# Newton steps through a PSUM bank, a second round in small pieces between shared steps, and the late table among the tiles

## The chip, the cores and the metric

The kernel runs on one core of one Trainium2 chip. Its metric is the device time of one execution, in microseconds. A core has five engines with queues of their own: TensorE (PE), VectorE (DVE), ScalarE (ACT), GpSimd (POOL) and SyncE (SP), the last used for DMAs. Each works through its instructions in the order in which they are written and waits only on semaphores.

## What is computed

One pre-norm transformer layer on 2048 tokens of width 128:

```
x = x + attention(layernorm(x))        # 16 heads of 64, causal, softmax, output projection
x = x + ffn(layernorm(x))
ffn(x): shared = (silu(x @ sg.T) * (x @ su.T)) @ sd.T
        probs = softmax(x @ gate_w.T); topw, topi = top_k(probs, 2); topw /= topw.sum
        out = shared + sum over the two chosen of 8 experts of topw * expert(x)
```

The hidden width of every expert is 352. The kernel keeps the accuracy of fp32 by splitting numbers into a high and a low part, so a product is three matmuls (`mm3`).

## The kernel before

**Attention.** Each of 16 heads has 20 slots, one for each pair of key tiles of a block of 512 queries. A slot n is: scores on TensorE into `st`, two exponentials on ScalarE (fp32 and fp16), `p_low` on GpSimd (L583, the difference of the two), and on TensorE the products with v of slot n - 3. `exps(n)` waits until products n - 5 are done, scores n until exponentials n - 2 are. `normalise` on VectorE ends a block (slots 1, 5, 11, 19), and the first product of the next block waits for it. Between scores and products each slot takes *background tasks*, each on TensorE into one of three banks `bg`, drained by VectorE in the same order (`bg_ready`, `bg_drained`). `LAST_HEAD` places those of head 15: `att_t`/`att_y` (output projection of a block), `turn` (tokens to partitions, statistics), `rows_t` (normalised rows back), `logits`. Their consumers on VectorE are `inverse_deviation` (reciprocal root by two Newton steps, operations of 8 elements, lines L805 to L816), `normal_rows` (L824) and `second_copy` (a copy of the rows for the second expert).

**Router.** Twice, for 1024 tokens each: ScalarE's exp, `router_top` (L849 to L867), `router_weights`, `ranks` and `places` (where each row goes). Then GpSimd's `scatter_rows` writes the rows of that half to memory, sorted by expert, with 16 indirect DMAs (L611).

**Shared expert.** Twelve steps q: two times three products into `st`, silu on ScalarE, `hidden` (L1064) on VectorE, high part on ScalarE, low part `hidden_lo` (L1070) on VectorE, and `down` of step q - 2 on TensorE (L1152 to L1154 are the products). Between the steps the rest of the last head's tasks, the second round of the router and the tables stand in an order written by hand. `early_table` gives the rows and experts of tiles 0 to 8, which need the first scatter only, `late_table` those of the other 30.

**Tiles.** 39 tiles of 128 rows of one expert: SyncE gathers (L498), TensorE transposes (L1393), makes six products (L1403 to L1408), transposes silu's product (L1417) and multiplies down (L1426, L1430); VectorE and ScalarE work between; GpSimd stores each result (L618). A gather waits for the store eight tiles before. At the end SyncE loads the stored rows (L503), VectorE adds them (L1143, L1145), SyncE stores the output (L507).

## Time and profile before

| | us |
|---|---|
| median of 3 runs (lowest, highest) | 1005.98 (1005.53, 1006.03) |
| profiled execution | 999.62 |
| its span | 997.8 |
| TensorE, VectorE, ScalarE, GpSimd busy | 935.9, 741.6, 713.4, 729.9 |
| mean granted TensorE clock (share of full) | 0.954 |

The profile is of one execution. Its times count from the start of the span. A row gives start, length, engine, line, operation and operands; an engine's idle time before the row and what ended it stand in square brackets. Instructions of one engine overlap a little, so the next can start before the row before it ends.

### The profile page before, as it was taken

Reading aid. Unit: us, or ns where it says so; the run is one execution under the profiler, and the core shown is the slowest. Engines: PE = TensorE matmul, PEld = TensorE weight load, DVE = VectorE, ACT = ScalarE, POOL = GpSimd, SP = SyncE. Lnnn points to the kernel's source line nnn. Section 1 sums busy time; section 2 is a strip of 40 time slices with the busy share of each in tenths; the row PEclk is TensorE's granted clock in tenths of the full one; section 3 lists DMA queues with packets and bytes.
Section 4 is the critical chain, followed back from the end, with each engine's and each line's share of the span. In section 5 each row is a group of like instructions: output and inputs, shape, how many; then the busy total and the mean of one; then the engine's idle time right before and its main releaser. Section 6 shows DMA issues by size and latency. Waiting matters only on the chain. (4 is left out here: it accounts for less than half of the span.)

```text
span 997.8 us, 25979 instructions
## 1 busy us (share of the span) xinstructions
PE 935.9 (94%) x10330; PEld 793.1 (79%) x10330; DVE 741.6 (74%) x1775; ACT 713.4 (71%) x891; POOL 729.9 (73%) x460
## 2 busy tenths in 40 slices
PE   7889999999999999999999999999999976679992
PEld 6558888888888888888888888888888765569992
DVE  4978696868778786878697869686876478656664
ACT  3038888888788788788878788888888853426661
POOL 1328878888888889888988897888789956154442
PEclk7769999999999999999999999999999979879996
DMA  3321434343534344444522241404030306011214
GB/s 104 84 53 34 94 77 115 80 108 77 117 78 108 79 116 94 110 89 112 108 75 66 75 93 41 111 29 102 1 87 5 133 6 249 25 49 57 58 55 134
DMA packets 70103, 82.03 MB, mean 82 GB/s; under 512 B 8784, under 2 KB 53970, under 8 KB 67936
## 3 DMA queue, kind: packets, MB, share of 16 engines
q1 hardware_dynamic: 67712, 76.14, 31.0%
q0 software_dynamic: 2272, 4.24, 1.2%
q8 instruction: 84, 1.38, 0.6%
q14 instruction: 35, 0.29, 0.1%
HBM read 21.81 MB, written 25.30 MB: 47 GB/s over the span
## 5 line engine op out<-in xcount | busy, mean ns | idle before, releaser
L583 POOL TENSOR_TENSOR p_lo<-prob,p_hi 128x1024 f16<-128x1024 f32 x320 | 617.2, 1947 | 144.8 <-ACT p_hi L685 143.5
L684 ACT ACTIVATE prob<-st,p_bias 128x1024 f32<-128x1024 f32 x320 | 330.0, 1031 | 131.2 <-PE st L1276 106.8
L685 ACT ACTIVATE p_hi<-st,p_bias 128x1024 f16<-128x1024 f32 x320 | 328.1, 1025 | 0.0
L979 DVE TENSOR_REDUCE row_max<-bg 128x1 f32<-128x512 f32 x384 | 255.7, 686 | 15.8 <-PE bg L1201 10.8
L1275 PE MATMUL st<-big 128*128 128x512 f32 (+3 forms) x640 | 246.8, 386 | 2.5 <-ACT p_hi L685 1.6
L1300 PEld LDWEIGHTS pv<-v_parts,p_hi 128*128 128x128 f16 x2176 | 198.1, 96 | 56.8 <-issue 33.3
L1201 PE MATMUL bg<-big 128*128 128x512 f32 (+3 forms) x640 | 240.2, 407 | 2.7 <-DVE v_parts L969 2.1
L1300 PE MATMUL pv<-v_parts,p_hi 128*128 128x65 f16 x2176 | 236.6, 195 | 1.8 <-POOL p_lo L583 1.8
L1276 PE MATMUL st<-big 65*128 65x512 f32 (+3 forms) x640 | 236.3, 369 | 0.0
L1302 PE MATMUL pv<-v_parts,p_hi 128*128 128x64 f16 x2176 | 234.1, 195 | 0.0
L1304 PE MATMUL pv<-v_parts,p_lo 128*128 128x65 f16 x2176 | 232.4, 192 | 0.0
L1304 PEld LDWEIGHTS pv<-v_parts,p_lo 128*128 128x128 f16 x2176 | 203.2, 99 | 0.0
L1302 PEld LDWEIGHTS pv<-v_parts,p_hi 128*128 128x128 f16 x2176 | 202.9, 97 | 0.1
L1201 PEld LDWEIGHTS bg<-big 128*128 128x128 f32 x640 | 122.4, 195 | 29.1 <-DVE row_max L979 7.5
L1275 PEld LDWEIGHTS st<-big 128*128 128x128 f32 x640 | 122.9, 192 | 17.5 <-ACT p_hi L685 2.8
L1276 PEld LDWEIGHTS st<-big 65*128 65x128 f32 x640 | 122.2, 191 | 16.5
L975 DVE CUSTOM_DVE_ANT_0 junk<-bg,mask_wide 128x128 bf16<-128x128 f32 (+3 forms) x256 | 122.1, 484 | 10.7 <-PE bg L1201 10.5
L959 DVE TENSOR_SCALAR big<-bg,qk_bias 128x512 fp32r<-128x512 f32 x64 | 48.0, 750 | 72.8 <-PE bg L1154 72.7
L618 POOL DMA_INDIRECT y_dram<-p_lo,v_parts x39 | 37.8, 970 | 46.6 <-DVE p_lo L1123 46.6
L1280 PE MATMUL st<-mask_cols_r,ident_r 128*128 128x128 f32 x256 | 61.1, 239 | 0.0
L1280 PEld LDWEIGHTS st<-mask_cols_r,ident_r 128*128 128x128 f32 x256 | 49.2, 192 | 2.8
L961 DVE SCALAR_TENSOR_TENSOR big<-bg,qk_bias,big 128x512 fp32r<-128x512 f32 x64 | 48.1, 751 | 2.3
(224 smaller groups left out, 1214.4 us busy)
## 6 DMA issues: line engine op xcount, KB each, us to landing
big<-big SPq DMA_DIRECT2D x192, 128.0 KB, 2.3
row_dram<-fill SPq DMA_DIRECT2D x8, 1300.0 KB, 9.2
big<-part_dram SPq DMA_DIRECT2D x8, 1088.0 KB, 7.9
big<-big SPq DMA_DIRECT2D x16, 512.0 KB, 4.3
part_dram<-stage_parts SPq DMA_DIRECT2D x32, 176.0 KB, 2.6
part_dram<-stage_parts SPq DMA_DIRECT2D x16, 192.0 KB, 3.7
stage_raw<-ffn_w SPq DMA_DIRECT2D x16, 176.0 KB, 3.0
v_parts<-row_dram SPq DMA_DIRECT2D x39, 65.0 KB
```

Of the source, the lines that this page charges most:

```text
L583: nc.gpsimd.tensor_tensor(o, a, b, ALU.subtract).then_inc(p_lo_ready, 1)
L684: nc.scalar.activation(o32, src, ACT.Exp, bias=p_bias[:], scale=D ** -0.5)
L685: nc.scalar.activation(o16, src, ACT.Exp, bias=p_bias[:], scale=D ** -0.5).then_inc(exp_done, 1)
L975: nc.vector.tensor_tensor_reduce(masked[k % BGRING][:, 0:width], bank[:, 0:width], mask_wide[:, BLK - width:BLK], 1.0, -3.0e38, ALU.add, A ...
L979: nc.vector.tensor_reduce(row_max[:, t, c:c + 1], bank, AX_X, ALU.max).then_inc(bg_drained, 1)
L1201: mm = nc.tensor.matmul(bank[:, 0:width], q_hihi[s][:, tile(t)], k_lohi[s][:, c * BLK:c * BLK + width], start=True, stop=True)
L1275: nc.tensor.matmul(out, k_lohi[s][:, tile(kt)], q_hihi[s][:, q], start=True, stop=False)
L1276: mm = nc.tensor.matmul(out, k_hi_one[s][0:D + 1, tile(kt)], q_lo_shift[s][0:D + 1, q], start=False, stop=not diagonal)
L1280: mm = nc.tensor.matmul(st[:, n % STRING, k, tile(j)], ident_r[:], mask_cols_r[:], start=False, stop=True)
L1300: nc.tensor.matmul(out, p_hi[:, n % PRING, cols], v[:, 0:D + 1], start=(kt == 0 and j == 0), stop=False, skip_group_check=True)
L1302: nc.tensor.matmul(out[:, 0:D], p_hi[:, n % PRING, cols], v[:, D + 1:VW], start=False, stop=False, skip_group_check=True)
L1304: mm = nc.tensor.matmul(out, p_lo[:, n % PRING, cols], v[:, 0:D + 1], start=False, stop=(kt == 4 * b + j), skip_group_check=True)
```

## The change

In words:
- The Newton steps write their squares and a copy of the operand into the bank of the last `turn`, so that each two-input operation has one input in PSUM; the bank is given back after them. `inverse_deviation` is called inside `turn` 1 and `turn` 3.
- In the last head `rows_t 0` and 1 go from slots 13 and 15 to 15 and 17, `second_copy` to 13 and 14, `logits 0` from 16 to 19, and `turn 2` comes from the shared stage into slot 18. `router_exps(0)` and `router_top(0)` come after the last slot, on VectorE behind the last `normalise`.
- In the shared stage the rows of blocks 2 and 3 are normalised by ScalarE, the low parts of steps 6, 7 and 8 are GpSimd's, between its two scatters, and tasks, copies and the early table stand at other steps. `base 2` comes before the last low part.
- The late table is cut into three pieces behind the first three tiles.
- Blocks 1 and 3 of the final loads and stores are issued by ScalarE's queue.

The diff, without declarations:

```diff
@@ -54,8 +54,8 @@
              9: [("att_t", PAIRS - 1, 1)], 10: [("att_y", PAIRS - 1, 1)], 11: [("turn", 1)],
-             13: [("rows_t", 0)], 15: [("rows_t", 1)], 16: [("att_t", PAIRS - 1, 2), ("logits", 0)],
-             17: [("att_y", PAIRS - 1, 2)]}
+             15: [("rows_t", 0)], 16: [("att_t", PAIRS - 1, 2)], 17: [("att_y", PAIRS - 1, 2), ("rows_t", 1)],
+             18: [("turn", 2)], 19: [("logits", 0)]}
 STAGE_SLOTS = (9, 15)
@@ -132,8 +132,9 @@
 PROLOGUE += [("v", 0, q) for q in range(4)] + max_tasks(0) + [("shift", 0)]
-TAIL = [("ranks", 0), ("att_t", PAIRS - 1, 3), ("att_y", PAIRS - 1, 3), ("turn", 2), ("turn", 3), ("rows_t", 2),
-        ("rows_t", 3), ("base", 0), ("logits", 1), ("base", 1), ("ranks", 1), ("base", 2), ("base", 3)]
+TAIL = [("ranks", 0), ("att_t", PAIRS - 1, 3), ("att_y", PAIRS - 1, 3), ("turn", 3), ("base", 0), ("rows_t", 2),
+        ("rows_t", 3), ("logits", 1), ("base", 1), ("ranks", 1), ("base", 2), ("base", 3)]
+POOL_LOW = (6, 7, 8)
 STAGED = [(e, j) for e in range(EXPERTS) for j in range(3)]
@@ -388,6 +394,13 @@
             return slice(8 * g, 8 * g + 8)
+
+        def wait_hidden_low(eng, q):
+
+            if q in POOL_LOW:
+                eng.wait_ge(h_lo_pool, POOL_LOW.index(q) + 1)
+            elif q >= 0:
+                eng.wait_ge(h_lo_ready, sum(x not in POOL_LOW for x in range(q + 1)))
@@ -621,9 +632,17 @@
+            def hidden_low(q):
+                pool.wait_ge(h_hi_ready, q + 1)
+                wait(pool, down_done, q - HRING + 1)
+                nc.gpsimd.tensor_tensor(h_lo[q % HRING], h32[q % HRING], h_hi[q % HRING], ALU.subtract
+                                        ).then_inc(h_lo_pool, 1)
+
             pool.wait_ge(filled, 16 * FILLS)
-            for g in range(2):
-                scatter_rows(g)
+            scatter_rows(0)
+            for q in POOL_LOW:
+                hidden_low(q)
+            scatter_rows(1)
             for i in range(TILES):
@@ -700,8 +719,6 @@
                     exps(h, n)
-                    if h == H - 1 and n == 17:
-                        router_exps(0)
                     if n in STAGE_SLOTS and 0 <= 2 * (h - STAGE_FROM) < len(STAGED):
@@ -721,6 +738,16 @@
+            def normal_rows(b):
+
+                act.wait_ge(ln_scale, 1)
+                act.wait_ge(bg_drained, drained(("turn", b)))
+                for t in range(4 * b, 4 * b + 4):
+                    last = nc.scalar.activation(attn[:, t, 0:P], res[:, tile(t)], ACT.Identity, bias=shift_mean[:, t - 8:t - 7],
+                                                scale=rstd[:, t:t + 1])
+                last.then_inc(ln_rows, 1)
+
+            router_exps(0)
             for q in range(STEPS):
@@ -728,9 +755,13 @@
                     shared_copy((q - 5) // FC)
-                if q in (4, 5):
-                    turned_copy(q - 2)
-                if q == 8:
+                if q == 4:
+                    normal_rows(2)
+                    normal_rows(3)
+                if q == 5:
+                    turned_copy(2)
+                    turned_copy(3)
+                if q == 7:
                     router_exps(1)
@@ -763,6 +794,14 @@
                     tile_y_low(i - 2)
+            for k in range(YRING):
+                act.wait_ge(y_stored[k], 16 * len(range(k, TILES, YRING)))
+            for b in (1, 3):
+                act.dma_start(y_rows[:, 4 * b:4 * b + 4], y_back[:, 4 * b:4 * b + 4]).then_inc(y_landed[b], 16)
+            for b in (1, 3):
+                act.wait_ge(out_ready, b + 1)
+                act.dma_start(out_view[:, 4 * b:4 * b + 4, :], res[:, blk(b)].rearrange("p (t d) -> p t d", d=P)
+                              ).then_inc(out_stored, 16)
@@ -808,14 +847,24 @@
                                             ALU.mult, ALU.add))
+                wide = bg[:, NUMBER["turn", 2 * g + 1] % BGRING, :]
+                square, copy = wide[:, 0:8], wide[:, 8:16]
                 y = newton[:, 1]
                 for k, step in enumerate(RSQRT_STEPS):
-                    own(nc.vector.tensor_tensor(newton[:, 0], y, y, ALU.mult))
-                    own(nc.vector.tensor_tensor(newton[:, 0], newton[:, 0], var_half[:], ALU.mult))
+                    own(nc.vector.tensor_copy(copy, y))
+                    own(nc.vector.tensor_tensor(square, copy, y, ALU.mult))
+                    own(nc.vector.tensor_tensor(square, square, var_half[:], ALU.mult))
                     out = newton[:, 2] if k == 0 else rstd[:, t]
-                    own(nc.vector.scalar_tensor_tensor(out=out, in0=newton[:, 0], scalar=step, in1=y,
-                                                       op0=ALU.add, op1=ALU.mult))
+                    last = nc.vector.scalar_tensor_tensor(out=out, in0=square, scalar=step, in1=y, op0=ALU.add,
+                                                          op1=ALU.mult)
+                    if k == 0:
+                        own(last)
                     y = out
+                last.then_inc(bg_drained, 1)
+                dve.wait_ge(bg_drained, drained(("turn", 2 * g + 1)))
+                if g:
+                    nc.vector.scalar_tensor_tensor(out=shift_mean[:], in0=mean_var[:, t, 0], scalar=-1.0, in1=rstd[:, t],
+                                                   op0=ALU.mult, op1=ALU.mult).then_inc(ln_scale, 1)
@@ -907,13 +956,15 @@
-            def table(lo, n):
-
+            def table_bases():
                 own(nc.vector.tensor_scalar(gap[:, EXPERTS:EXPERTS + 1], end_tile[:, EXPERTS - 1:EXPERTS], -1.0, None,
                                             ALU.mult))
                 own(nc.vector.scalar_tensor_tensor(out=row_base, in0=gap, scalar=float(P), in1=region[:], op0=ALU.mult,
                                                    op1=ALU.add))
                 own(nc.vector.tensor_tensor(row_step, row_base[:, 1:EXPERTS + 1], row_base[:, 0:EXPERTS], ALU.subtract))
+
+            def table(lo, n):
+
                 by = ends_by[:, 0:n]
@@ -928,23 +979,25 @@
-            def early_table():
+            def early_bases():
                 tiles_counted(ALU.is_ge, 1)
                 running_ends()
                 own(nc.vector.tensor_scalar(gap[:, 0:EXPERTS], first_tile, -1.0, None, ALU.mult))
                 own(nc.vector.tensor_scalar(taken, first_tile, -1.0, float(EARLY), ALU.mult, ALU.add))
                 own(nc.vector.scalar_tensor_tensor(out=taken, in0=taken, scalar=0.0, in1=n_tiles, op0=ALU.max, op1=ALU.min))
-                table(0, EARLY)
-
-            def late_table():
+                table_bases()
+
+            def late_counts():
                 dve.wait_ge(table_ready, 1)
                 tiles_counted(ALU.is_gt, 0)
                 own(nc.vector.tensor_tensor(n_tiles, n_tiles, taken, ALU.subtract))
                 running_ends()
+
+            def late_bases():
                 own(nc.vector.tensor_tensor(gap[:, 0:EXPERTS], taken, first_tile, ALU.subtract))
-                table(EARLY, TILES - EARLY)
+                table_bases()
@@ -997,11 +1050,15 @@
                     last.then_inc(ln_stats, 1)
-                    nc.vector.tensor_copy(res[:, blk(b)], bank).then_inc(bg_drained, 1)
+                    copied = nc.vector.tensor_copy(res[:, blk(b)], bank)
+                    if b % 2 == 0:
+                        copied.then_inc(bg_drained, 1)
                     dve.wait_ge(ln_stats, b + 1)
                     for t in range(4 * b, 4 * b + 4):
                         last = nc.vector.bn_aggr(mean_var[:, t, :], stats[:, t, :])
                     own(last)
+                    if b % 2:
+                        inverse_deviation(b // 2)
                 elif task[0] == "rows_t":
@@ -1047,20 +1104,16 @@
                         background_task(task)
-                    if h == H - 1 and n == 11:
-                        inverse_deviation(0)
-                        normal_rows(0)
-                    if h == H - 1 and n == 12:
-                        normal_rows(1)
-                    if h == H - 1 and n in (14, 17):
-                        second_copy(0 if n == 14 else 1)
+                    if h == H - 1 and n in (11, 12):
+                        normal_rows(n - 11)
+                    if h == H - 1 and n in (13, 14):
+                        second_copy(n - 13)
+            normalise(H - 1, NG - 1)
             router_top(0)
-            normalise(H - 1, NG - 1)
             router_weights(0)
-            background_task(("ranks", 0))
             def hidden(q):
                 dve.wait_ge(silu_done, q + 1)
-                wait(dve, h_lo_ready, q - HRING + 1)
+                wait_hidden_low(dve, q - HRING)
                 nc.vector.tensor_tensor(h32[q % HRING], silu[q % SRING], st[:, q % 2, 1, :], ALU.mult
@@ -1072,39 +1125,36 @@
                 hidden(q)
-                if q:
+                if q and q - 1 not in POOL_LOW:
                     hidden_lo(q - 1)
                 if q == 0:
+                    background_task(("ranks", 0))
                     background_task(("att_t", PAIRS - 1, 3))
                 if q == 1:
                     background_task(("att_y", PAIRS - 1, 3))
                 if q == 2:
-                    background_task(("turn", 2))
                     background_task(("turn", 3))
                 if q == 3:
-                    inverse_deviation(1)
-                    normal_rows(2)
-                    normal_rows(3)
+                    early_bases()
                 if q == 4:
+                    table(0, EARLY)
+                if q == 5:
+                    background_task(("base", 0))
                     background_task(("rows_t", 2))
-                if q == 5:
                     background_task(("rows_t", 3))
+                if q == 6:
+                    background_task(("logits", 1))
                     second_copy(2)
+                if q == 7:
                     second_copy(3)
-                if q == 6:
-                    background_task(("base", 0))
-                    background_task(("logits", 1))
-                if q == 7:
-                    early_table()
                 if q == 8:
                     background_task(("base", 1))
                     router_top(1)
                 if q == 9:
                     router_weights(1)
                     background_task(("ranks", 1))
+            background_task(("base", 2))
             hidden_lo(STEPS - 1)
-            background_task(("base", 2))
-            late_table()
             background_task(("base", 3))
@@ -1137,6 +1187,12 @@
                     tile_y(i - 2)
+                if i == 0:
+                    late_counts()
+                if i == 1:
+                    late_bases()
+                if i == 2:
+                    table(EARLY, TILES - EARLY)
             for b in range(NB):
@@ -1361,22 +1417,20 @@
                     ).then_inc(gu_ready, 1)
+                if q == 2:
+                    background_task(("att_y", PAIRS - 1, 3))
                 if q >= FLAG:
                     down(q - FLAG)
-                if q == 0:
+                if q == 1:
                     background_task(("ranks", 0))
                     background_task(("att_t", PAIRS - 1, 3))
-                if q == 1:
-                    background_task(("att_y", PAIRS - 1, 3))
                 if q == 2:
-                    background_task(("turn", 2))
                     background_task(("turn", 3))
-                if q == 4:
+                if q == 5:
+                    background_task(("base", 0))
                     background_task(("rows_t", 2))
-                if q == 5:
                     background_task(("rows_t", 3))
                 if q == 6:
-                    background_task(("base", 0))
                     background_task(("logits", 1))
```

## Rows read from the trace of the kernel before

**Rows 1.** Stretches: busy us of each engine (instructions), clock, DMA share, GB/s.
```profile
782.00:826.20 44.20, 34.90 (x470) 29.55 (x469) 30.47 (x94) 29.69 (x32) 30.77 (x16) 0.88 0.08 28
826.20:892.50 66.30, 45.72 (x210) 35.53 (x206) 46.50 (x174) 20.75 (x36) 27.39 (x27) 0.85 0.28 101
892.50:985.20 92.70, 86.63 (x623) 83.68 (x622) 57.07 (x155) 53.62 (x155) 43.42 (x45) 0.96 0.18 52
```

**Rows 2.** Waits, 780 to 830 us: who waited for whom, total us, times, longest.
```profile
POOL p_lo L583 <- ACT p_hi L685: 13.0, 6, 7.9
...
PE bg L1228 <- DVE attn L824: 6.2, 1, 6.2
```

**Rows 3.** GpSimd in order of time, last head: start us, us, instruction [idle before].
```profile
795.16 3.26 POOL L583 TENSOR_TENSOR p_lo<-prob,p_hi 128x1024 f16<-128x1024 f32 x2 [1.27 <-ACT p_hi L685]
799.59 4.21 POOL L583 TENSOR_TENSOR p_lo<-prob,p_hi 128x1024 f16<-128x1024 f32 x2 [1.17 <-ACT p_hi L685]
811.65 6.47 POOL L583 TENSOR_TENSOR p_lo<-prob,p_hi 128x1024 f16<-128x1024 f32 x3 [7.85 <-ACT p_hi L685]
...
822.66 3.24 POOL L583 TENSOR_TENSOR p_lo<-prob,p_hi 128x1024 f16<-128x1024 f32 x2 [0.40 <-ACT p_hi L685]
```

**Rows 4.** VectorE in order of time, the first deviation's Newton steps.
```profile
797.45 0.99 DVE L805 TENSOR_SCALAR var_half<-mean_var 128x8 f32<-128x8 f32 x1
...
799.77 1.98 DVE L813 TENSOR_TENSOR newton<-newton 128x8 f32<-128x8 f32 x1
801.78 2.04 DVE L814 TENSOR_TENSOR newton<-newton,var_half 128x8 f32<-128x8 f32 x1
...
804.06 2.14 DVE L824 TENSOR_SCALAR attn<-res,mean_var,rstd 128x128 f32<-128x128 f32 x8
```

**Rows 5.** VectorE in order of time: router rounds, then the late table.
```profile
820.72 1.62 DVE L851 TENSOR_TENSOR pr<-pr,pr_sum 128x64 f32<-128x64 f32 x1
...
868.27 0.21 DVE L849 TENSOR_REDUCE pr_sum<-pr 128x8 f32<-128x64 f32 x1
...
886.53 0.28 DVE L897 SCALAR_TENSOR_TENSOR wo_all<-w_raw,iota_row 128x128 f32<-128x128 f32 x1
...
891.25 0.68 DVE L1020 TENSOR_TENSOR res<-res,bg 128x512 f32<-128x512 f32 x1
```

**Rows 6.** One source line: minimum, median and maximum ns of one instruction.
```profile
L824 DVE TENSOR_SCALAR attn<-res,mean_var,rstd x16: 331/340/586, 804.1 to 846.6; 128x128 f32<-128x128 f32 x16
```

**Rows 7.** TensorE in order of time, shared stage and start of the tiles.
```profile
834.79 0.39 PE L1152 MATMUL st<-xn_hi,shared_hi 128*128 128x512 f32 x1
...
835.49 0.40 PE L1152 MATMUL pv<-split,shared_hi 128*128 128x512 f32 x1
...
872.47 0.56 PE L1243 MATMUL bg<-wo_all,tri 128*128 128x64 f32 x2 [3.69 <-issue]
...
892.28 0.45 PE L1393 MATMUL pv<-ident,v_parts 128*128 128x128 f32 x1 [2.62 <-DVE shared_hi L1112]
```

**Rows 8.** VectorE in order of time, first tiles; then the end.
```profile
897.15 0.52 DVE L1132 TENSOR_TENSOR prob<-prob,st 128x352 f32<-128x352 f32 x1 [1.25 <-ACT prob L759]
...
898.55 0.52 DVE L1132 TENSOR_TENSOR prob<-prob,st 128x352 f32<-128x352 f32 x1 [0.22 <-ACT prob L759]
...
901.07 0.52 DVE L1132 TENSOR_TENSOR prob<-prob,st 128x352 f32<-128x352 f32 x1 [0.77 <-ACT prob L759]
...
989.21 0.69 DVE L1143 TENSOR_TENSOR res<-res,big 128x512 f32<-128x512 f32 x1 [6.87 <-DMA big<-y_dram]
```

**Rows 9.** GpSimd in order of time: second scatter's first instruction, first tile's store.
```profile
879.03 0.97 POOL L611 DMA_INDIRECT row_dram<-attn,place_u  x1 [25.24 <-DVE place_u L893]
...
901.09 0.97 POOL L618 DMA_INDIRECT y_dram<-p_lo,v_parts  x1 [1.47 <-DVE p_lo L1123]
```

**Rows 10.** SyncE's queue in order of time, from 884 us: start us, us, issues.
```profile
904.05 64.84 SPq L498 DMA_DIRECT2D v_parts<-row_dram  x31
985.37 2.03 SPq L503 DMA_DIRECT2D big<-y_dram  x4
```

12 lines of the change are left out of this document (7 added, 5 removed).

## The prediction

> **What bounds the kernel now.** I read the table of stretches first, then the waits around the last head, then each engine in order of time. The profiled execution took 999.62 us, of which 997.8 are the span; the runs have a median of 1005.98, 6.4 above it. All terms below are differences worked out from the one trace, and I subtract their sum from both totals alike.
>
> The change touches nothing before 797 us, slot 11 of the last head. Three stretches are open [rows 1]: the end of the last head (44.2 us, TensorE busy 34.9, its mean granted clock 0.88), the shared expert (66.3 us, busy 45.7, clock 0.85), and the tiles (92.7 us, busy 86.6). So TensorE bounds the tiles alone. In the last head GpSimd sets the pace, since a full p_low takes it 2.1 us (two in 4.21) without a pause when it is fed; and it sat idle for 13.0 us waiting for exponentials, 7.9 of them at once [rows 2, 3]. Behind that lies one chain: the Newton steps hold up `normal_rows`, TensorE stands 6.2 us in slot 13 before the transposes of `rows_t 0` [rows 2], no scores are made, ScalarE and then GpSimd run dry. The reader is to see why the steps are long: eight-element operations take 0.17 us, but L805 took 0.99 and ended when GpSimd's operations of 795.16 did (798.42), L813 took 1.98 and L814 2.04, each ending as one of the two of 799.59 ended [rows 3, 4]. The same happens to L851 in the first router round, 1.62 us [rows 5]. I read it as VectorE waiting for a GpSimd instruction to let go of the memory side they share.
>
> The page "SBUF — State Buffer" of the Trainium skill, section "Who interferes with whom", says so: a VectorE operation with two SBUF inputs, or a copy or tensor_scalar in a two-port mode, is fully blocked by a GpSimd instruction that reads SBUF, for that instruction's length. The trace agrees, with the numbers above. The rule also speaks against this change: it leaves the copies and tensor_scalars from SBUF to SBUF exposed, which is the first rival below.
>
> **Last head.** Newton's products now have one input in a PSUM bank. Each of the two rounds of steps costs one extra copy of 0.2 us, so eight operations, 1.6 us, where six took 4.9 (three of 0.2 before 799.77, then until 804.06); L805's 0.99 stays. `normal_rows(0)` starts at 800.8 instead of 804.06. `rows_t 0` goes from slot 13 to 15, so scores 14 and 15 are issued before it: exponentials 12 and 13 allow them (GpSimd had both by 801.7, the second of its operations of 799.59), and GpSimd's operations 14 and 15 run from 803.8 to 808.1 without the 7.85 us hole [rows 3]. What VectorE must finish next is `normal_rows` 0 and 1 (eight L824, 2.14 together [rows 4]), two `second_copy` (0.6 each), then `normalise` of block 2 (0.6), for which the product of slot 15 waits. Four cases of this:
> If nothing is held by GpSimd, they end by 804.8, GpSimd loses 0.65 us, and its last operation ends at 817.5 instead of 825.9 [rows 3]; the stage ends near 818.1, 8.1 us earlier than 826.2.
> If each L824 waits out one GpSimd operation, four of them take until 808.1, when GpSimd has no more input; the rest follows at its free speed, block 2 is normalised at 811.0, scores 16 come at 812.8, GpSimd goes on at 814.9 and the stage ends at 822.9: 3.3 us earlier, at worst 2.5 if the clock falls again as it did after the 6.2 us stall.
> The L824 have no wait between them, last 0.34 each and start 0.26 apart (eight in 2.14) [rows 4, 6], so the next has begun before the last is over. If they thus pass as one batch, GpSimd loses 2.1 us for the eight L824 and about one more for the copies, and block 2 is normalised at 807.7; with scores 16 at 809.5 GpSimd's operations 16 to 19 end by 819.2: 6.7 us earlier.
> If PSUM operands wait as well, it is as in the second case. I take 6.0, between the first three, and keep 2.5 and 8.1. `turn 2` and `logits 0` in slots 18 and 19 cost TensorE 2.3 us under GpSimd's pace; they would be on the path only if GpSimd were no longer the bound. The exponentials of the router leave this stage's ScalarE for nothing.
>
> **Shared expert.** I walk it from its first product (826.24 before), as offsets. The lengths are six products 1.4, three 0.7 (834.79 to 835.49 at the high clock), a full-width VectorE operation 0.6 to 0.7, a router top free of GpSimd 4.1 (868.27 to the ranks' start at 872.47) [rows 5, 7].
> Lost: `router_top(0)` used to run under the last p_lows and now comes after the last `normalise`; with its weights VectorE is free at 5.7 instead of 2.0. TensorE waits for it at 4.7 (ranks 0 are behind the second step now); attention's transposes and products follow to 10.5, against 7.8 before.
> Won: one `turn` (1.8 us of VectorE) has left the stage, and eight L824 (2.4 us, until 846.9) are ScalarE's. The walk gives `turn 3` at 12.2, its Newton steps until 17.3, ScalarE's rows until 20.6 (0.27 each), and sixth step at 20.8 against 23.4. From here each step waits for the low part of the one before it: down 3 at 23.2, base 0 and both `rows_t` until 25.5, their ScalarE and VectorE copies until 27.9, logits 1 until 30.6. Two hidden parts before the router are GpSimd's; its first scatter ends at 8.3 + 20.6 = 29, before they are asked for at 33, so they hide. ScalarE's exp stands one step earlier, so its two table loads delay step 8's silu to 36.7; down 6 is issued at 37.9, as before (38.0). `router_top(1)` ends at 43.9 instead of 46.2: 2.3 us won. I bound this walk by plus 1.6 and minus 2.3 (nothing won), its largest unproved piece (down 2 waits at 18.7 for VectorE behind `turn 3`, 3 us of idle TensorE in which the clock may fall; its mean in this stage was 0.85 [rows 1]).
> Behind it the order is ranks 1, two steps, the last downs. The late table, 886.53 to 891.25, stands between the last low part and VectorE's answer to the first tile; TensorE waited 2.62 us for that before the tile of 892.28 [rows 5, 7]. It is worth 4.7 if all of it is on the path (the last downs and `base 3` run beside it, so 3.1 at least); `base 2` ahead of the last low part gives some 0.9 more: 5.6 for both, 3.1 the low bound. Stage: 2.3 + 5.6 = 7.9 won; bounds 3.1 and 9.5. The first tile's product is then at offset 58.4 instead of 66.3.
>
> **Tiles.** The table's three pieces are 1.6, 0.8 and 2.3 us (its 4.7 split by their six, four and seven operations and widths) [rows 5]. VectorE's idle time in the first three iterations was 1.25, 0.22 and 0.77 [rows 8]: VectorE lags 0.3, then 0.9, then 2.5 us, and TensorE, which had no more than some 0.5 us of room, gets most of it as a stall: 2.3. Low bound 0.5 (all room used), high 4.7 (all of it). Behind the table on VectorE stands tile 2's silu product, and TensorE waits for that.
> On GpSimd the second scatter stands ahead of all tile stores. Places come at offset 48.0; 0.8 + 20.6 us later (879.03 to 899.62, 1.47 before the store of 901.09) [rows 9] it is 69.4. The first tile's result, 8.6 us after the first product (892.5 to 901.09) plus 2.3, is ready at 69.3: about together. GpSimd was idle 1.47 us there before; that room is gone. SyncE's ninth gather waits for that store and went out at 904.05 [rows 10], 3.0 us behind it; any lateness of the store is the gather's. I take 0.5 for it, 0 to 2.0. Tiles: 2.8 lost.
>
> **End.** Two of four loads of y and of the stores leave from ScalarE's queue. The chain is: first load issued at 985.37, VectorE adding from 989.21 [rows 8, 10]. The first load leaves no earlier; what can be saved is SyncE's 0.5 us per issue (four in 2.03), which already hides behind the transfers. What can be lost is that load 1 shares the engines with load 0 from the start: up to 1.4 us, a third of the 3.8 from its issue to the first addition. I take 0.7 lost, bounds 0.3 won and 1.4 lost. The page "DMA: Bandwidth & Descriptors", section "Issuing engines are not separate DMA queues", says in the Trainium skill that such DMAs interleave on the same 16 engines whoever starts them and that only issue time is saved; by it the term would be a loss, as taken. No run here shows it yet.
>
> **Sum.** 6.0 + 7.9 - 2.8 - 0.7 = 10.4 us won: the profiled time 999.62 becomes 989.2, the median 1005.98 becomes 995.6. All bounds at once: 8.1 + 9.5 - 0.5 + 0.3 = 17.4 won, or 2.5 + 3.1 - 6.7 - 1.4 = 2.5 lost.
>
> **Rivals.** (A) L824 and the copies wait one by one for GpSimd, or PSUM inputs do too, so that the Newton edit buys little: last head 3.3, total 7.7 won, 998.3. For it: L813 and L814, one after the other, each waited a whole operation [rows 4]; against: they have a semaphore wait between them and the L824 haven't. (B) The table gives everything back among the tiles and the first store waits 2 us: tiles lose 6.7, total 6.5 won, 999.5. For it: TensorE is busy 93% there, and so has no room [rows 1]; against: the start of the tiles has gaps.
> (C) The slower side: the second scatter becomes the bound. From the ninth tile on rows come from it, and the result of the first can't be stored before it. It decides from the point where places 1 come more than 10 us after the offset of 48.0, that is after 58, for instance because GpSimd's three low parts and VectorE wait for each other in steps 6 to 9; each us beyond is a us on the end, at 64 the time is 1011. In the trace places 1 came 14.3 us before the first tile's product (0.8 before the scatter of 879.03, against 892.5) [rows 1, 9], and the walk has 10.4.
>
> **Chances.** Forecast (8.5 to 17) 0.55; A 0.22; B 0.13; C 0.05; all small terms cancelling to within 2 us, 0.05. A measurement here can tell 0.2%, 2.0 us, from no change. That gives faster 0.90, same 0.05, slower 0.05. Eight in ten: 989.5 (16.5 won) to 1002.5 (3.5 won), which takes in A and B.
>
> **What would show it.** The forecast's steps: L813's successors at 0.17 us each while GpSimd is busy; TensorE's wait for L824 in the last head under 2 us; GpSimd's idle time there from 13.0 to below 5; first shared product near 820; no wait for hot_ready longer than 3 us; first tile product 58 after it; y stores starting 11 us after that; first y load landing a little later than 3.8 us after its issue. Wrong would be: single L824 of 2 us (A), first tiles 2.1 us apart becoming 4 (B), a long GpSimd wait for places 1 (C), or a new wait of TensorE behind steps 3 to 5 of the shared stage.

## The result, and the profile after

The changed kernel takes 1015.85 us (median of 8 runs, 1012.08 to 1020.15), the kernel before on the same chip 1006.00 (8 runs). The ratio is 1.0089, 95% interval 1.0067 to 1.0111: 9.9 us slower, where 10.4 us faster was forecast. The profiled execution of the changed kernel took 1013.28 us, span 1011.5.

Its stretches, with the bounds at the same events as in [rows 1] (columns: stretch, its length, busy us of TensorE, its weight loads, VectorE, ScalarE and GpSimd, then clock, DMA share, GB/s):

```profile
782.00:824.50 42.50, 33.88 (x462) 28.98 (x458) 28.86 (x75) 28.33 (x30) 29.29 (x16) 0.88 0.07 25
824.50:897.00 72.50, 48.03 (x204) 37.33 (x200) 42.57 (x169) 23.75 (x44) 29.05 (x29) 0.83 0.26 94
897.00:998.00 101.00, 90.74 (x623) 85.49 (x622) 61.00 (x172) 53.79 (x155) 44.27 (x46) 0.92 0.16 48
```

The shared expert has 72.5 us instead of 66.3 and the tiles 101.0 instead of 92.7. Of the 1.7 us by which the first stretch is shorter, 1.4 lie ahead of the change (the transposes of `turn 1` start at 793.6, before at 795.0). VectorE in order of time, the Newton steps that answer to [rows 4]:

```profile
796.02 1.00 DVE L844 TENSOR_SCALAR var_half<-mean_var 128x8 f32<-128x8 f32 x1
...
797.95 0.17 DVE L855 TENSOR_TENSOR bg<-bg,newton 128x8 f32<-128x8 f32 x1
798.16 0.17 DVE L856 TENSOR_TENSOR bg<-bg,var_half 128x8 f32<-128x8 f32 x1
...
799.39 8.27 DVE L873 TENSOR_SCALAR attn<-res,mean_var,rstd 128x128 f32<-128x128 f32 x8
```

The two Newton products that took 1.98 and 2.04 take 0.17 each. But the eight `normal_rows` operations behind them take 8.27 us instead of 2.14. One source line (minimum, median, maximum ns of one), GpSimd in order of time, and who waited in the stretch:

```profile
L873 DVE TENSOR_SCALAR attn<-res,mean_var,rstd x8: 332/662/2178, 799.4 to 807.3; 128x128 f32<-128x128 f32 x8
```

```profile
798.16 8.39 POOL L594 TENSOR_TENSOR p_lo<-prob,p_hi 128x1024 f16<-128x1024 f32 x4 [1.16 <-ACT p_hi L704]
814.81 2.15 POOL L594 TENSOR_TENSOR p_lo<-prob,p_hi 128x1024 f16<-128x1024 f32 x1 [8.26 <-ACT p_hi L704]
817.88 2.14 POOL L594 TENSOR_TENSOR p_lo<-prob,p_hi 128x1024 f16<-128x1024 f32 x1 [0.92 <-ACT p_hi L704]
820.82 3.25 POOL L594 TENSOR_TENSOR p_lo<-prob,p_hi 128x1024 f16<-128x1024 f32 x2 [0.80 <-ACT p_hi L704]
```

```profile
POOL p_lo L594 <- ACT p_hi L704: 12.7, 6, 8.3
...
PE bg L1284 <- DVE attn L873: 5.4, 1, 5.4
```

Taken one by one, the operations last 0.99, 2.18, 2.16 and 2.16 us, each ending as one of GpSimd's four operations of 798.16 ended; the last four, 0.33 us each, start 0.25 us apart from 806.56 on, when GpSimd has run dry. GpSimd's idle time has moved (8.26 where it was 7.85), not gone. From `turn 1` to the first shared product it is 30.9 us, before 31.2.

ScalarE in the middle of the shared stage, then TensorE there:

```profile
847.35 0.58 ACT L739 COPY p_lo<-pv 128x512 f32<-128x512 f32 x1
856.51 0.58 ACT L673 COPY xn<-bg 128x512 f32<-128x512 f32 x1 [8.58 <-remote]
```

```profile
849.90 1.91 PE L1284 MATMUL bg<-ident,attn 128*128 128x128 f32 x8
858.52 0.77 PE L1208 MATMUL st<-xn_hi,shared_hi 128*128 128x512 f32 x1 [6.71 <-DVE xn_lo L1069]
```

TensorE has turned the rows by 851.8, but ScalarE takes its copy of them up at 856.51, 4.7 us later (the first 3.9 of its 8.58 idle us it waits for TensorE), and the releaser that the profile finds is none of the engines' own ("remote"). VectorE in the same time:

```profile
849.40 0.23 DVE L976 TENSOR_REDUCE w_raw<-wo_all 128x9 f32<-128x72 f32 x1 [0.47 <-DVE wo_all L974]
850.12 0.17 DVE L977 SCALAR_TENSOR_TENSOR w_raw<-iota_row,w_raw 128x9 f32<-128x9 f32 x1 [0.49 <-DVE w_raw L976]
...
854.35 0.69 DVE L1077 TENSOR_TENSOR res<-res,bg 128x512 f32<-128x512 f32 x1 [2.10 <-issue]
```

L977 needs only L976, which is its own engine's and took 0.23, and starts 0.49 us behind it, where L856 above starts 0.04 behind L855. The same is seen at the start of the tiles (ScalarE, then GpSimd):

```profile
907.73 0.46 ACT L790 ACTIVATE prob<-st 128x352 f32<-128x352 f32 x1 [4.68 <-remote]
```

```profile
904.30 0.97 POOL L622 DMA_INDIRECT row_dram<-p_hi,place_u  x1 [0.30 <-issue]
912.86 0.97 POOL L629 DMA_INDIRECT y_dram<-p_lo,v_parts  x1 [7.58 <-DVE p_lo L1173]
```

I call this *late starts*: TensorE, VectorE and ScalarE begin instructions some tenths of a microsecond to 4.7 us after what they wait for. The ScalarE row of 907.73 had its input since TensorE's six products ended at 900.5 and its engine free since 903.05. GpSimd's 7.58 us are not a late start of its own; it waits for VectorE's result, which is late. The late starts stand from 847 to 858 and from 899 to 908; GpSimd issues its scatters of rows from 833.8 to 854.4 and from 885.1 to 905.3, so each group begins under a scatter and ends some 3 us behind it. The end (SyncE, then VectorE; [rows 8, 10]):

```profile
997.99 0.93 SPq L515 DMA_DIRECT2D big<-y_dram  x2
```

```profile
1002.91 0.69 DVE L1199 TENSOR_TENSOR res<-res,big 128x512 f32<-128x512 f32 x1 [7.95 <-DMA big<-y_dram]
```

4.9 us from the first load to the first addition, before 3.8.

**All traces in one table.** Differences of starts, us: from the transposes of `turn 1` to the first shared product; from there to the first tile product; to the first store of y; to the last one; to the end of the span. "Ratio" is against the kernel before on the same chip, from all runs of both; the other columns are of one execution each. The kernels come below.

| kernel | head | shared | to 1st y | tiles | end | span | ratio (95%) |
|---|---|---|---|---|---|---|---|
| before, profile shown ahead | 31.2 | 66.3 | 8.6 | 82.0 | 14.6 | 997.8 | |
| before, again (e5) | 31.2 | 66.2 | 13.9 | 83.1 | 14.7 | 1004.2 | |
| changed | 30.9 | 72.5 | 15.9 | 82.9 | 15.8 | 1011.5 | 1.0089 (1.0067-1.0111) |
| changed, again (e1) | 31.2 | 72.8 | 15.6 | 83.5 | 15.8 | 1013.8 | 1.0058 (1.0037-1.0079) |
| e2 Newton alone | 29.8 | 70.4 | 14.0 | 84.2 | 14.8 | 1008.5 | 0.9988 (0.9972-1.0003) |
| e3 late table alone | 30.0 | 68.4 | 15.0 | 84.5 | 14.6 | 1007.0 | 0.9997 (0.9978-1.0016) |
| e4 two queues alone | 30.9 | 68.0 | 13.5 | 83.9 | 15.7 | 1006.4 | 1.0004 (0.9987-1.0022) |
| e6 before, no scatter | 30.4 | 67.0 | 9.2 | 81.6 | 14.7 | 996.1 | 0.9917 (0.9889-0.9946) |
| e7 changed, no scatter | 30.4 | 66.7 | 8.6 | 83.5 | 15.6 | 1000.3 | 0.9940 (0.9919-0.9961) |
| e8 changed, low parts on VectorE | 30.2 | 74.6 | 16.7 | 83.7 | 15.8 | 1016.5 | 1.0059 (1.0038-1.0080) |
| e9 changed, no first scatter | 31.1 | 68.1 | 14.5 | 83.2 | 15.7 | 1007.6 | 1.0008 (0.9992-1.0023) |
| e10 changed, no second | 30.9 | 72.6 | 9.3 | 83.0 | 15.7 | 1005.7 | 1.0014 (0.9995-1.0034) |
| e11 as e7, table and end as before | 31.0 | 69.3 | 8.4 | 82.1 | 14.8 | 999.2 | 0.9936 (0.9911-0.9962) |
| e12 changed, rows from PSUM | 31.1 | 72.8 | 15.2 | 83.3 | 15.8 | 1013.4 | 1.0091 (1.0059-1.0122) |
| e13 before, no first scatter | 30.2 | 67.1 | 13.2 | 84.5 | 14.7 | 1003.0 | 0.9956 (0.9933-0.9978) |
| e14 before, no second | 31.0 | 68.0 | 9.0 | 81.9 | 14.7 | 998.7 | 0.9908 (0.9879-0.9937) |
| e15 changed, exps a step later | 30.8 | 71.2 | 15.2 | 82.8 | 15.7 | 1011.1 | 1.0034 (1.0014-1.0054) |
| e16 e2 and rows from PSUM | 30.0 | 69.0 | 15.6 | 81.5 | 14.9 | 1006.0 | 0.9994 (0.9974-1.0015) |
| e17 before, half of the scatters | 30.6 | 67.4 | 9.0 | 81.4 | 14.9 | 999.4 | 0.9994 (0.9977-1.0011) |
| e18 changed, table and end as before | 30.4 | 68.1 | 8.2 | 82.8 | 14.6 | 999.0 | 0.9993 (0.9973-1.0013) |

Stretches of unchanged code differ from trace to trace by 1 to 2 us: the head of the kernel before is 31.2 in its two traces, 30.0 in e3 and 30.2 in e13, which leave the head alone, and its shared stage is 66.2 in e5 and 68.0 in e4, which changes only the end. A difference of that size between two traces is a hint, not a measurement.

### The profile page after: what moved, and what is told of

The parts are those of the page before. It is cut to its first block, busy times and chain, and to the rows that moved or that the text cites. A ratio compares the mean times of both kernels' runs of the same rounds, so it can differ in the third digit from the quotient of the medians.

```text
span 1011.5 us, 25993 instructions
## 1 busy us (share of the span) xinstructions
PE 940.3 (93%) x10330; PEld 795.3 (79%) x10330; DVE 739.8 (73%) x1769; ACT 716.4 (71%) x899; POOL 732.2 (72%) x463
## 3 DMA queue, kind: packets, MB, share of 16 engines
q10 hardware_dynamic: 2112, 1.57, 0.5%
## 4 chain that ended last, share of the span: by engine, by line
PE 82%; DVE 6%; issue 4%; DMA 3%; ACT 2%; another core or an unknown queue 1%; SPq 1%; POOL 0%; POOLq 0%; DVEq 0%; ACTq 0%
PE bg L1257 14%; PE st L1331 13%; PE st L1332 12%; PE pv L1356 7%; PE pv L1358 6%; PE pv L1360 6%; PE bg L1208 3%; PE bg L1247 3%; PE bg L1209 2%; PE bg L1210 2%; PE st L1336 2%; PE bg L1267 2%; DVE row_max L1032 1%; PE bg L1480 1%
## 5 line engine op out<-in xcount | busy, mean ns | idle before, releaser
L1032 DVE TENSOR_REDUCE row_max<-bg 128x1 f32<-128x512 f32 x384 | 255.6, 685 | 15.7 <-PE bg L1257 10.9
L1257 PEld LDWEIGHTS bg<-big 128*128 128x128 f32 x640 | 122.0, 194 | 29.8 <-DVE row_max L1032 7.8
L1012 DVE TENSOR_SCALAR big<-bg,qk_bias 128x512 fp32r<-128x512 f32 x64 | 48.0, 749 | 72.5 <-PE bg L1210 72.5
```

The lines of the kernel that those rows point to most:

```text
L1032: nc.vector.tensor_reduce(row_max[:, t, c:c + 1], bank, AX_X, ALU.max).then_inc(bg_drained, 1)
L1257: mm = nc.tensor.matmul(bank[:, 0:width], q_hihi[s][:, tile(t)], k_lohi[s][:, c * BLK:c * BLK + width], start=True, stop=True)
```

## The experiments

**The parts alone, and the changed kernel again (e1 to e4, one chip).** e1 is the changed kernel; the others are the kernel before with one part of the change.

```
e2   own(nc.vector.tensor_copy(copy, y))            # copy, square: 8 columns of turn 1's bank
     own(nc.vector.tensor_tensor(square, copy, y, ALU.mult))
e3   -            late_table()                      # ahead of base 3
     +  i == 0: late_counts()   i == 1: late_bases()   i == 2: table(EARLY, TILES - EARLY)
e4   loads and stores of blocks 1 and 3 from ScalarE's queue
```

> The changed kernel itself, for a second trace. Its first trace holds two stretches (847 to 857 and 901 to 908 us) in which VectorE and ScalarE start instructions late though what they wait for is there. Theory P (the placement brings the stretches): they come again at the same work, and the time is about 1.009 of before. Rival N (they fell into one trace by chance): this trace lacks them and its span is some 10 us shorter, while the time over rounds stays 1.009, so that the loss must lie elsewhere.

> The kernel before, with the Newton products through the bank alone. Theory: the two waits of 2 us behind GpSimd go, normal_rows(0) starts 3.3 us earlier while GpSimd is still busy, so some of its eight operations wait for GpSimd instead; rows_t 0 starts 1 to 3 us earlier: 1 to 3 us faster (ratio 0.997 to 0.999). Rival (each operation of normal_rows waits out one GpSimd operation in its turn): no gain, ratio 1.000 within 0.001.

> The kernel before, with the late table in three pieces behind the first three tiles and nothing else changed. Theory of the prediction: 4.7 us won before the tiles, 2.3 lost among them, 1.5 to 2.5 us faster (ratio 0.998). Rival (the first store and the ninth gather are bound by the end of the second scatter, which does not move): the tiles start 4.7 earlier and lose it all, ratio 1.000 to 1.002.

> The kernel before, with blocks 1 and 3 of the final loads and stores on ScalarE's queue. Theory: the first load shares the DMA engines and lands up to 1.4 us later, end 0.7 to 1.4 us later (ratio 1.001). Rival (only issue time is saved): 0.3 to 0.5 us faster, ratio 0.9995.

e1 came to 1015.72, and its trace has the late starts at the same work again (ScalarE's copy of turned rows behind 8.25 us of idle time, "remote"). e2 came to 1009.44, e3 to 1009.07, e4 to 1010.13, with 1010.03 for the kernel before beside them. The gains expected of e2 (1 to 3 us) and e3 (1.5 to 2.5) are not seen. So no part by itself costs or wins what can be told from nothing; the loss belongs to what is left, the order of head and shared stage, or to the parts together. e4's trace has the 1.0 us at the end (15.7 against 14.7), e3's 1.4 more among the tiles (84.5 against 83.1), but e2, which leaves the table alone, has 84.2 there. e2's trace has Newton's edit by itself:

```profile
801.02 4.59 DVE L831 TENSOR_SCALAR attn<-res,mean_var,rstd 128x128 f32<-128x128 f32 x8
```

The eight `normal_rows` operations start earlier and take 4.59 us instead of 2.14, beside GpSimd's two operations of 799.79. They end 10.4 us after the transposes of `turn 1`, before 11.2 [rows 4]: of the 3.3 us that the Newton steps give, 0.8 is left.

**The scatters (e5 to e7, one chip, with e8).** The late starts stood beside GpSimd's scatters of rows, so these were left out of both kernels. The rows then never reach `row_dram`, and the tiles work on its fill values; y is filled with zeros ahead of the tiles. e5 is the kernel before once more.

```
-  for t in range(8 * g, 8 * g + 8):                # in scatter_rows(g)
+  for t in range(0):
```

> The kernel before, for a second trace. Its first one spans 997.8 us, while the traces of three kernels that differ from it in one small part span 1006.4 to 1008.5 and start their first store 13 to 15 us after the first tile product instead of 8.6. Theory P (engines start late while GpSimd's scatter is under way, in this kernel too, and the first trace happened to be free of it): span 1004 to 1009, first store some 13 us after the first product. Rival: 998 and 8.6 again, so that each of the three edits brings the delay by itself.

> The kernel before without the scatter of the rows (both halves): the tiles read the filled list, their results are dropped, and y is filled once in an earlier stage. Its time is the time of the chain alone. Theory P: the late starts go, 5 to 9 us faster than before (0.991 to 0.995). Rival (the scatter costs nothing but its own waits): within 2 us.

> The changed kernel without the scatter of the rows, as in the run before it. Theory P (its loss is that its critical work stands beside the scatters): it gains 12 to 16 us and comes out equal to the kernel before without scatter or up to 3 us faster than that. Rival (the loss is in its order of the work): it stays 6 to 9 us slower than the kernel before without scatter.

e6: 997.81 (before beside it 1006.78), e7: 1001.46. Leaving out 32 DMAs of 128 short rows, for which TensorE, VectorE and ScalarE are not seen to wait, wins 9 us in the one kernel and 14.4 in the other (1015.85 to 1001.46, on different chips). Against e1 beside its own kernel before, the second number is 12 thousandths instead of 15. So the scatters account for some 4 to 6 of the ten microseconds. The other 3.7 us, e7 against e6, were expected to be nothing; they are not clear of noise, since the two ratios' intervals overlap (0.9919 to 0.9961 and 0.9889 to 0.9946).

e5 shows why the forecast knew nothing of it. Against the profile from which I forecast, its instructions start within 0.1 us of the same times (read from 846 to 862 and from 892 on) until the second tile; then ScalarE and VectorE read, in e5

```profile
895.06 0.26 ACT L741 CAST shared_hi<-pv 128x128 fp32r<-128x128 f32 x1
900.35 0.46 ACT L759 ACTIVATE prob<-st 128x352 f32<-128x352 f32 x1 [5.02 <-PE st L1408]
```

```profile
900.84 0.52 DVE L1132 TENSOR_TENSOR prob<-prob,st 128x352 f32<-128x352 f32 x1 [4.92 <-issue]
```

where [rows 8] has VectorE's operation at 897.15. TensorE too, between two products of one tile, with no wait between them in the code:

```profile
897.63 0.43 PE L1406 MATMUL st<-big,shared_hi 128*128 x1
898.97 0.40 PE L1407 MATMUL st<-big,shared_hi 128*128 x1 [0.92 <-issue]
```

The first y store follows at 906.42 instead of 901.09 [rows 9], and the span is 6.4 us longer: just what the first profile lay under its median.

e8 moved the three low parts of the shared expert back from GpSimd to VectorE in the changed kernel.

```
-POOL_LOW = (6, 7, 8)
+POOL_LOW = ()
```

> The changed kernel with all low parts of the hidden values on VectorE, none on GpSimd. Theory: GpSimd's three (1.3 us each against 0.7) end at 868.2, 872.2 and 878.2 and make down 6 wait for nothing, since silu's table holds it to 871.4 anyway, but one of them holds VectorE's L912 for 1.2 us: without them 0 to 1 us faster, ratio to before 1.005 to 1.008. Rival (the three hold the chain): 2 to 4 us faster than the changed kernel, ratio to before 1.003.

1013.45, ratio 1.0059 (1.0038 to 1.0080), where the changed kernel has 1.0058 to 1.0089: they are at most a small part of the loss.

**Which scatter (e9, e10 on one chip; e13, e14 on another).** The same edit for g = 0 or g = 1 alone; the rows of the other half of the tokens are scattered as always.

> The changed kernel with the first of its two scatters of rows (blocks 0 and 1) left out, so these rows are never written and their outputs are wrong in value; y is filled with zeros earlier. Leaving out both took 14.4 us (1015.85 to 1001.46). Theory 1, the loss sits in the shared stage: the late starts at 847 to 858.5 fall on the copies of the turned rows, on the path there, so this one is worth 6 to 8 us: 1008 to 1010, ratio to before 1.001 to 1.003, shared stage 66 to 68 instead of 72.5, its end before the first tile. Theory 2, the loss sits in the second scatter, which stands over the start of the tiles and before the first store: this one is worth under 3 us, 1013 or more, shared stage above 70.

> The changed kernel with the second of its two scatters (blocks 2 and 3) left out, output wrong in those rows. Theory 1: it is worth what the stretch from the first tile product to the first store shows, 15.9 against 8.6 us, so 6 to 7.5: 1008.5 to 1010, and the first shared stage stays at 72 to 73. Theory 2 (the second scatter alone makes the loss): 1003 or less. If the sum of both single savings is below 12 us, the two hide each other in part; if it is 14, they add up.

> The kernel before with the scatter of blocks 0 and 1 left out (its rows are never written, output wrong there). Leaving out both gave 0.9917 of before. In the changed kernel the first scatter alone is worth 7.4 us (1015.85 to 1008.4) and shows as a shared stage of 68.1 instead of 72.5. Theory 1: in the kernel before the first scatter runs earlier, beside attention's transposes and the slack behind them, so it is worth under 1.5 us: ratio 0.9985 to 1.0, shared stage 66 to 67, and the difference in this scatter is what the change lost by moving ranks 0 later. Theory 2: each scatter costs the same in both kernels, some 4 here: 0.996, and the second costs 4 as well.

> The kernel before with the scatter of blocks 2 and 3 left out (output wrong there). Theory 1: nearly all of the 8.3 us that both scatters cost is this one's, ratio 0.9925 to 0.9940, and the stretch from first tile product to first store is 9 instead of 13.9. Theory 2: half of it, 0.996.

In the changed kernel the first is worth 8.3 thousandths (from 1.0091 of e12, a near copy of the changed kernel on the same chip, to 1.0008) and the second 7.7; both are clear of noise. Each shows where it stands: without the first the shared stage is 68.1 instead of 72.5, without the second the way to the first y store is 9.3 instead of 15.9. My two theories were not rivals; both hold. ScalarE in e9, for the 856.51 above:

```profile
848.75 0.58 ACT L745 COPY p_lo<-pv 128x512 f32<-128x512 f32 x1
852.00 0.59 ACT L679 COPY xn<-bg 128x512 f32<-128x512 f32 x1 [2.67 <-PE bg L1290]
```

In the kernel before the first is worth 4.4 thousandths (2.2 to 6.7) and the second 9.2. The second was thus dear before as well. That the first became dearer by the new order is what the traces say; the two ratios alone don't settle it, for 8.3 is itself uncertain by more than 3, and in the kernel before the two single savings add up to 13.6 on one chip where leaving out both gave 8.3 on another. Six traces with the old order and both scatters have 66.2 to 70.4 us of shared stage (before, e5, e2, e3, e4, and 69.0 in e16 below); five with the new one have 71.2 to 74.6 (changed, e1, e8 with 74.6, e12, e15). Without the first scatter it is 67.1 (e13) and 68.1 (e9). In the old order ScalarE's copy of turned rows at 847.20 started on time in both traces of the kernel before (847.27 in e5) and so did the next at 854; in e4 and e14 this second copy was late too, behind 4.20 and 4.13 us of idle time instead of 2.61. In the new order the copies of both blocks come in one group, due at 851.8, in the last 2.6 us of the scatter. That this place is what makes them dearer is argued, not tried. The expectation of under 1.5 us for e13 was missed.

**What is left without scatters (e11).** e7 with the late table ahead of `base 3` again and one queue at the end.

```
+  late_counts(); late_bases(); table(EARLY, TILES - EARLY)
   background_task(("base", 3))
```

> The changed kernel without both scatters (output wrong), and in it the late table again ahead of the tiles and the loads and stores of the end again on one queue. Without the scatters the changed kernel was 3.7 us slower than the kernel before (1001.46 against 997.81, ratios 0.994 and 0.9917). If the table among the tiles and the two queues make all of it, this one comes to 0.9917 to 0.9925 of before, 998 to 998.5, with 81.6 from first to last store and 14.7 after it. If the late table in front costs its 4.7 us in the shared stage, as my forecast had it, the stage grows by 3 to 5 and the time stays at 1001 to 1003.

1000.95 against e7's 1001.46: nothing. In the table of traces the shared stage is 2.6 longer, the tiles are 1.4 shorter, the way to the first store 0.2 and the end 0.8. The second theory was the better one, with 2.6 for the table where it had 3 to 5. So table and end are not the 3.7 us. Against e6, e11 has 69.3 instead of 67.0 in the shared stage, which would make the new *order* of that stage cost 2.3 where the walk won 2.3; e18 and e17 below put it at 0.7 (68.1 against 67.4). What holds is that no trace shows the order winning anything.

**The order's own cost (e15).**

```
-  if q == 7:
+  if q == 8:
       router_exps(1)
```

> The changed kernel with the second round's router exponentials one step later on ScalarE, behind silu 8 and shared_copy(1), where the kernel before has them. Theory 1: the table loads ahead of silu 8 hold up shared_copy(1) and so down 6, 3.6 us of TensorE's waiting; moved, down 6 comes 2.5 to 3 earlier, router_top(1) starts at 47 instead of 50 (offset in the shared stage), and the stage is 70 instead of 72.5: 1013 to 1013.5. Theory 2: the exponentials themselves are then late, router_top(1) waits for them and the time stays at 1015.5 to 1016.

Ratio 1.0034, with 1009.70 for the kernel before; the changed kernel had 1.0058 beside a kernel before of 1010.03 and 1.0089 beside 1006.00. That is 2.4 us or more, clear of noise against the second of these but not against the first, and the stage has 71.2 instead of 72.5. In the changed kernel ScalarE reads

```profile
866.86 1.28 ACT L685 ACT_TABLE_LOAD   x1
868.15 0.26 ACT L685 ACTIVATE pr<-lg 128x64 f32<-128x64 f32 x1
868.42 1.28 ACT L753 ACT_TABLE_LOAD   x1
869.72 0.60 ACT L753 ACTIVATE prob<-st 128x512 f32<-128x512 f32 x1
870.21 0.61 ACT L733 CAST split<-prob 128x512 fp32r<-128x512 f32 x1
870.72 0.59 ACT L739 COPY p_lo<-pv 128x512 f32<-128x512 f32 x1
```

```profile
867.41 0.39 PE L1210 MATMUL st<-xn_hi,shared_lo 128*128 128x512 f32 x1
871.41 0.47 PE L1208 MATMUL pv<-split,shared_hi 128*128 128x512 f32 x1 [3.61 <-issue]
```

TensorE's down 6 stands 3.61 us until `shared_copy(1)` (870.72) is over, and this stands behind exponentials with two table loads.

**The last head (e12, e16).** Three of the four rows of block 1 are normalised from the PSUM bank of `turn 1`, not from the copy in `res`; e12 in the changed kernel, e16 in e2.

```
+  for j in (1, 2, 3):
+      nc.vector.tensor_scalar(attn[:, 4 + j, 0:P], wide[:, tile(j)], mean_var[:, 4 + j, 0:1],
+                              rstd[:, 4 + j:5 + j], ALU.subtract, ALU.mult)
```

> The changed kernel with three of the eight normal_rows operations of the last head reading the product's PSUM bank instead of the SBUF copy in res; the other five as they are. Theory 1, an operation whose wide input is in PSUM is not held by GpSimd: these three take about 0.3 us each, the other five about one GpSimd operation each (1.0), so the group ends 2.5 us earlier and the last head is up to 2.5 us shorter (28.5 instead of 30.9), 1013.5. Theory 2, the output to SBUF or the small SBUF scalars are enough to be held: all eight still take about 1.03 each and nothing moves, 1015.8. Theory 3, held or not, the head is bound elsewhere (exponentials and scores behind block 2): the three are short and the head stays at 30.5 to 31.

> The kernel before with Newton's products in a PSUM bank and three of the eight normal_rows operations of the last head reading the product's bank. The Newton part alone gave 0.9988 (0.9972 to 1.0003). The three take 0.35 each beside GpSimd; only block 0's operations (SBUF) still wait, for what is left of two GpSimd operations. Expected: the transposes of rows_t 0 start 0.3 to 0.5 us earlier, 0.998 to 0.9985 of before. If it stays at 0.9988 or above, the PSUM rows are worth nothing where block 0 has to come first anyway.

e12, VectorE in order of time:

```profile
801.01 1.05 DVE L866 TENSOR_SCALAR attn<-bg,mean_var,rstd 128x128 f32<-128x128 f32 x3
802.10 6.74 DVE L878 TENSOR_SCALAR attn<-res,mean_var,rstd 128x128 f32<-128x128 f32 x5
```

The three run beside GpSimd in 1.05 us; of the other five three take 2.07 to 2.16 and two 0.33. GpSimd's next four operations end at 808.24, the five at 808.84. So the operations with the wide input in PSUM were not held, but those that read SBUF still end only when GpSimd runs dry, and the head stays at 31.1: theory 3, for a reason that it didn't name. 1014.75, ratio 1.0091. e16: 1008.29, ratio 0.9994 (0.9974 to 1.0015): nothing either, and with e2's 0.9988 no gain of Newton through PSUM is shown in the runs. The head is 30.0 and 29.8 in these traces, but it is 30.0 in e3 too, which has the old Newton steps.

**A chip without late starts (e17, e18).** e17 is the kernel before with only the rows of first choice scattered (8 DMAs a round; the other rows are never written). e18 is the changed kernel with table and end as before.

```
e17  -  for r in range(2):      +  for r in range(1):       # in scatter_rows
```

> The kernel before with only the rows of the first choice scattered: 8 scatter DMAs instead of 16 in each of the two rounds (the rows of the second choice are never written, output wrong there), 10 us instead of 20.6 of scattering each. Leaving all out gave 0.9917, leaving out only the second round 0.9908. Theory 1: every instruction that starts while a scatter is under way can be late, so the cost goes with the time under scatter: 4 to 5 us saved, 0.995 to 0.996, the second round's ends at 890 before the first tile and the stretch from first tile product to first store is 9 to 10. Theory 2: the lateness comes once at the end of a scatter, whatever its length: about 1.0, and the late start stands 10 us earlier in the trace.

> The changed kernel with the late table ahead of the tiles again and the end on one queue again; the head, the order of the shared stage and both scatters as in the change. Without scatters these two undone parts together were worth nothing (1000.95 against 1001.46). Theory 1: the same here, 1.007 to 1.009 of before, since the table in front costs the shared stage 2.6 us and gives 1.6 back in the tiles and 0.9 at the end. Theory 2: with the scatter under way the tiles' start is where everything is late, and the table in front of it pushes the tiles' start behind the scatter, so that it comes out cheaper: 1.002 to 1.005.

These two ran on a chip on which the kernel before took 999.98 us (23 runs, 997.04 to 1005.87), where the four other chips of the experiments had 1006.78 to 1010.03. e17: 1000.34, ratio 0.9994. e18: 1000.14, ratio 0.9993. Neither trace has a late start (9.0 and 8.2 us to the first store), though e18 has all its scatters. So e17 tells nothing of what a scatter's lateness goes with, and neither of e18's theories was tried under its condition. What they do show: with both scatters under way but no late starts, the new order with the old table and end is as fast as the kernel before, within 2 us or so, and leaving out half of the scatters wins nothing. The changed kernel itself was not run on this chip.

## Why the prediction was wrong

The forecast was -6.0 head, -7.9 shared, +2.8 tiles, +0.7 end. Against e5, a trace of the kernel before that has its late starts, the changed kernel has -0.3, +6.3, +1.8 (2.0 to the first store, -0.2 behind it) and +1.1: +8.9 in sum. Nearly all of the 19 us between this and the forecast are in two terms.

**Last head 6.0: the step that failed is "If they thus pass as one batch".** The Newton steps did what was predicted: eight operations at 0.17 us where six had taken 4.9. But the L824 (L873 now) that follow are not a batch; the first four each wait until a GpSimd operation ends. That is the second of the four cases and rival A's mechanism, which I priced at 3.3. The rows bear the mechanism out: block 2 was normalised by 809.2, which is 810.6 on the time scale of the kernel before (`turn 1` was 1.4 earlier), forecast 811.0. What was mis-sized is the rest. GpSimd went on at 816.2 on that scale instead of 814.9. In TensorE's 5.4 us of waiting its clock fell; from 806 to 814.4 it was granted at 0.50, the low level. The four products of slot 16's scores (from 810.53) took 0.63 to 0.77 us each and 2.1 in all, where those of slot 17 (from 814.47, at 1.00) took 0.39 to 0.47 and 1.2 in all. That is 0.9 of the 1.3 us. GpSimd's last four operations then took 9.3 us and not 7.5, with 0.92 and 0.80 of waiting for exponentials, which themselves waited for the scores of slots 17 and 18; ahead of the latter stand the attention product of block 2 and the second `rows_t` (815.48 to 816.8), which the change put together in slot 17. Why the head is no shorter than before was not tried part by part: e2's 29.8 against 30.9 would let the reordering eat what Newton gives, but e3's 30.0 takes the force from it. The page "SBUF — State Buffer" of the Trainium skill, section "Who interferes with whom", gave the rule against my choice, that such an operation is held for the whole length of GpSimd's; the trace agrees, with 2.16 beside 2.14.

**Shared expert 7.9: the cost of a scatter was put at nothing, and the walk won nothing.**
"Its first scatter ends at 8.3 + 20.6 = 29 ... so they hide" counted a scatter as GpSimd's time alone. That time was nearly right (it ended 29.9 after the first product), but with both scatters this stage is 72.5 where it is 66.7 without (e7), and 4.4 of these 5.8 us go with the first scatter by e9. (By e10, which has the first alone and 72.6, all of them do.)
The walk's 2.3 us won are 0.7 to 2.3 lost by the pairs of traces above. Where the first scatter is away (e9) it was nearly right as far as the turned copies: down 3 at 23.3 (forecast 23.2), the copies done at 28.7 (27.9). Its first failing step is "logits 1 until 30.6": in e9 they end at 33.2, and in the kernel before at 32.5. The six products of step 6 start 0.43 us apart instead of the 0.235 assumed, at a granted clock of 0.50 (854.0 to 856.7; 1.00 until 850, where TensorE had just waited 2.29 us), which makes 1.2 us, and the logits themselves take 1.7 us. Step 8's silu is then at 38.9 (forecast 36.7), late by no more than that, and down 6 at 40.6 (37.9): the two table loads also hold `shared_copy(1)`, which I had not queued behind them. Moving the exponentials behind it made the stage 1.3 us shorter in e15. Then `router_top(1)` took 5.3 us to the ranks' start instead of 4.1, since one of its operations took 1.57 beside GpSimd's low part.
The late table is worth 2.6 by e11 against e7, not the 5.6 of table and `base 2`: even the low bound of 3.1 was too high. That the last downs and `base 3` run beside it is the likely reason and was not tried. With the scatters e3 shows no gain at all (68.4 where e5 has 66.2).

**Tiles 2.8.** The table costs 1.4 (e7 against e11) where 2.3 was forecast. The first store did get late, but not by the store queue: GpSimd had ended its scatter at 905.3 and waited 7.58 us for VectorE. Late starts cost 6.6 there (9.3 in e10 to 15.9), of which the kernel before pays 4.9 (9.0 in e14 to 13.9 in e5).

**End 0.7** was right: the end is 15.6 to 15.8 in every trace with two queues and 14.6 to 14.9 in every one with one. By the page "DMA: Bandwidth & Descriptors" of the Trainium skill, section "Issuing engines are not separate DMA queues", no time but that of the issue is saved; the traces agree, with 1.0 us lost instead of any saved.

Rival C named the right object, the second scatter, and the wrong mechanism. Its condition came true: the places of the second round were there 59.9 us after the first product, where 48.0 was forecast and 58 was its limit. But GpSimd was then waiting for VectorE and not the other way round. Its price was wrong too: at 64 its own rule of 1 us for each beyond 58 gives 995.6 + 6 = 1001.6, not 1011.

The prediction did see that its trace lay 6.4 us under the median of the runs, and took the sum from both alike. This is the error behind the errors: most of the gap was late starts that this one trace didn't show (e5 has 5.3 us more to the first store), and the change came to pay more of them. The account of the traces: late starts 5.8 + 1.7 = 7.5, order 2.3 (0.7 by the other pair), table -2.6 + 1.4, end 1.0, head -0.3, together 9.3 (7.7) beside the 8.9 measured. With 1 to 2 us of spread in each stretch that such a sum comes out is in part luck.

**Open.** What makes the late starts. They were not seen without a scatter of rows (e6, e7); they were absent from e18's trace, with the same scatters, on a chip where the kernel before is fast (999.98), and from the single execution from which I forecast, though the runs beside it were 6 us longer. That execution, 999.62 us, is none of those three runs, and on what chip it was taken is not on record: it would fit the fast chip. The changed kernel was not run there. Further, in e5 only one scatter of two had them. That the instructions themselves reached the engines late is unlikely: the DMA view of the changed kernel shows no transfer of an instruction queue from 847 to 858 or from 899 to 908. Whether they go with the number of scatter DMAs, their rows or the time was not tried on a chip that has them.

## What to carry to other kernels

When the profiled execution is faster than every run behind the median, find out what those runs pay before you price a change from it, and take a second trace on another chip. An engine freed from waiting runs into the next instruction of the same kind: name the successor and price it by the same rule as the one removed. When an activation of another table is moved on ScalarE, list everything queued behind it, not just the next silu.
